# Seams and one product: a vision kernel whose setup work is moved and whose first MLP product takes its variance another way

## The reference

```python
x = x + block0(groupnorm(x)); x = x + block1(groupnorm(x))
# block 0: windowed attention, then an MLP with a depthwise 5x5 convolution
y   = layernorm(tok) * norm1_w + norm1_b             # over the 96 channels of each pixel
tok = attention(y) + tok                             # 16x16 windows, step 14, 4 heads
...
y = (x2 - mean(x2)) / sqrt(var(x2) + 1e-5) * norm2_w + norm2_b   # over 96 channels
y = gelu(y @ fc1_w + fc1_b)                          # 96 -> 192
y = y + gelu(depthwise_conv5x5(y) + dw_b)
x1 = y @ fc2_w + fc2_b + x2                          # 192 -> 96
# block 1: each pixel of a region joins the nearest of 4 centres in each of 4 heads
f, v = conv1x1(x1, f_w), conv1x1(x1, v_w)
...
out = conv1x1(weighted per-head mean of v over each centre's pixels, spread back, proj_w)
```

## Time and profile before

| | us |
|---|---|
| median of 3 runs | 6937.62 (6933.67 to 6956.9) |
| the profiled execution, its own time | 6937.03 |
| its span | 6935.3 |
| PE busy in the span | 6015.5 (87%) |
| DVE busy | 5209.9 (75%) |
| ACT busy | 3497.3 (50%) |
| POOL busy | 2286.0 (33%) |

### The profile page before, as it was taken

The page is one execution under the profiler, slowest core; times in us unless marked ns, Lnnn a source line. Parts: engine busy times, 40 slices in busy tenths (PEclk is TensorE's granted clock), DMA queues, the critical chain, the costliest instruction groups (busy, mean ns, idle before and its releaser), DMA issues. The chain is left out here.

```text
span 6935.3 us, 135783 instructions
## 1 busy us (share of the span) xinstructions
PE 6015.5 (87%) x51768; PEld 3118.6 (45%) x51768; DVE 5209.9 (75%) x7712; ACT 3497.3 (50%) x5182; POOL 2286.0 (33%) x4080
## 2 busy tenths in 40 slices
PE   0885999999999999999999689989998666578887
PEld 0332555555555555555555233335555111066663
DVE  7686888888888888888888455558887445456666
ACT  0553666666666666666666356644443111144431
POOL 0343455555554555555554656610000000000000
PEclk9997999999999999999999799999999788789987
DMA  7786344444444444444443598888987999835667
GB/s 306 192 240 179 72 106 101 101 104 106 103 108 100 103 109 102 105 101 101 107 96 71 146 269 235 237 288 345 345 341 266 283 314 316 249 90 167 189 183 248
DMA packets 761666, 1252.65 MB, mean 181 GB/s; under 512 B 159364, under 2 KB 477828, under 8 KB 730948
## 3 DMA queue, kind: packets, MB, share of 16 engines
q1 hardware_dynamic: 700532, 1090.77, 55.8%
q10 hardware_dynamic: 54560, 111.50, 5.3%
q0 software_dynamic: 5936, 41.68, 1.7%
HBM read 680.81 MB, written 508.40 MB: 171 GB/s over the span
## 5 line engine op out<-in xcount | busy, mean ns | idle before, releaser
L801 DVE TENSOR_REDUCE at_mz<-at_ps 128x4 bf16<-128x1024 f32 x1444 | 1772.3, 1227 | 105.3 <-PE at_ps L720 80.3
L668 ACT ACTIVATE at_E<-at_ps 128x1024 f32<-128x1024 f32 x1444 | 1399.4, 1021 | 382.6 <-PE at_ps L732 368.0
L732 PE MATMUL at_ps<-at_qaug,at_k 32*128 32x256 f32 x11552 | 830.0, 401 | 23.7 <-DVE at_qaug L842 23.7
L743 PE MATMUL at_ps<-at_E,at_vaug 128*32 128x256 f32 x11552 | 774.3, 385 | 5.5
L1282 PE MATMUL cv_ps<-cv_yin,cv_band 128*128 128x384 f32 x2304 | 745.4, 486 | 26.2 <-DMA cv_yin<-y_mlp 26.2
L1302 DVE TENSOR_TENSOR cv_yin<-cv_gl,cv_yin 64x384 f32<-64x384 f32 x1152 | 637.6, 553 | 150.3 <-ACT cv_gl L1293 142.4
L732 PEld LDWEIGHTS at_ps<-at_qaug,at_k 32*128 32x128 f32 x11552 | 523.0, 184 | 494.1 <-issue 384.5
L590 POOL TENSOR_TENSOR at_share<-at_rden,t_share 128x8 f32<-128x8 f32 x722 | 148.5, 206 | 1445.5 <-DVE at_rden L812 1445.5
L1282 PEld LDWEIGHTS cv_ps<-cv_yin,cv_band 128*128 128x128 f32 x2304 | 436.1, 189 | 335.7 <-DMA cv_yin<-y_mlp 27.1
L720 PE MATMUL at_ps<-at_k,at_q 32*128 32x256 bf16 x5776 | 574.2, 275 | 8.9 <-DMA at_k<-at_packed 7.4
L1293 ACT ACTIVATE cv_gl<-cv_ps,cv_bias 128x384 f32<-128x384 f32 x576 | 335.1, 582 | 435.8 <-PE cv_ps L1282 435.8
(11 more groups left out here) (217 smaller groups left out, 9596.0 us busy)
## 6 DMA issues: line engine op xcount, KB each, us to landing
cv_yin<-y_mlp SPq DMA_DIRECT2D x48, 2340.0 KB, 14.8
s_mlp<-cv_yin SPq DMA_DIRECT2D x48, 2340.0 KB, 8.4
at_rows_in<-y_attention SPq DMA_DIRECT2D x76, 768.0 KB, 6.1
gn_xin<-in_x SPq DMA_DIRECT2D x16, 3072.0 KB, 23.2
ln_xin<-in_x SPq DMA_DIRECT2D x192, 256.0 KB, 7.4
y_attention<-ln_xin SPq DMA_DIRECT2D x192, 256.0 KB, 3.8
cl_xu<-x SPq DMA_DIRECT2D x128, 384.0 KB, 3.6
at_xr<-in_x SPq DMA_DIRECT2D x68, 672.0 KB, 5.7
```

The costliest lines, as they stand in the source:

```text
L668: act.activation(E[:, m % 2, 2 * p:2 * p + 2, :], psum[:, 2 + 2 * p:4 + 2 * p, :], ACT.Exp).then_inc(exp_done, 1)
L732: i = pe.matmul(psum[:, 2 + h, TOK * j:TOK * j + TOK], k[rows, n % 2, tokens(w, 128 * j, 128)], qaug[rows, m % 2, :], start=True, stop=True)
L743: i = pe.matmul(pv_ps[32 * h:32 * h + VC, 0:TOK], vaug[:, m % 2, z, h, :], E[:, m % 2, h, z * TOK:(z + 1) * TOK], start=(z == 0), stop=(z ...
L801: dve.tensor_reduce(mz[:, m % 2].rearrange("p j (h c) -> p h j c", c=32)[:, 2 * p:2 * p + 2, :, DQ], psum[:, 0:2, :].rearrange("p h (j n) ...
```

## The change

At the start, the statistics use the norm's ring (six buffers, `norm_tables`), the norm's first four tiles are loaded into it by the statistics' queue, the weights are loaded on ScalarE's queue meanwhile, the first image's aggregation comes right after its tiles, and scale and shift are spread by three matmuls with a spread identity instead of 24 transfers. In `fc1` the weights' loads move to ScalarE's queue; the weights are centred once (each column's mean over the channels is subtracted), so that x needn't be; the mean comes from one matmul on the sum of the three slices, made by VectorE; POOL squares the raw x; and the variance is the mean square less the squared mean, which ScalarE makes. In `fc2` the final waits go (the next block's sync engine waits instead), and the setup's loads and memsets run there on POOL's queue; `cluster_setup` makes the centres in 8 VectorE instructions and 8 POOL copies, and shares the last copies with ScalarE and POOL.

```diff
@@ group_norm_statistics @@
             for m in range(STEPS):
...
-                if m >= NBUF:
-                    sp.wait_ge(taken, m - NBUF + 1)
+                if m >= XB:
+                    sp.wait_ge(taken, m - XB + 1)
+                sp.dma_start(xin[:, m % XB, :], src[:, part * CH:(part + 1) * CH]).then_inc(loaded[m % XB], 16)
+            for k in range(LN_AHEAD):
+                sp.wait_ge(taken, STEPS + k - XB + 1)
+                norm_load(sp, x, s, k)
...
+            act.wait_ge(cleared, 4)
+            for to, of in setup_weights(p, t, s):
+                act.dma_start(to, of).then_inc(s["weights_loaded"], 16)
...
-            dve.wait_ge(taken, STEPS)
-            for b in range(B):
-                n = PART * PER
-                dve.bn_aggr(t["mean_var"][:, b, :], stats[:, b * n:(b + 1) * n, :]).then_inc(aggregated, 1)
+                if m % PART == PART - 1:
+                    b, n = m // PART, PART * PER
+                    dve.wait_ge(taken, m + 1)
+                    dve.bn_aggr(t["mean_var"][:, b, :], stats[:, b * n:(b + 1) * n, :]).then_inc(aggregated, 1)
@@ attention_setup @@
+            for grp in range(CGRP):
+                m = pe.matmul(ps[:, 3, 4 * grp:4 * grp + 2 * B], s["spread"][:, grp, :], t["gn"][:].rearrange("p a b -> p (a b)"), start=True, stop=True)
...
+                link(dve.tensor_copy(s["affine"][half], ps[half, 3, 0:4 * CGRP].rearrange("p (s a b) -> p a s b", a=2, b=B)[:, :, :, b]))
@@ layer_norm @@
-            for grp in range(CGRP):
-                for g in range(4):
-                    for to, of in ((scale, t["gn_scale"]), (shift, t["gn_shift"])):
-                        sp.dma_start(to[32 * g:32 * g + 32, grp:grp + 1], of[32 * grp:32 * grp + 32, g // 2:g // 2 + 1]).then_inc(w_loaded, 16)
...
-            for k in range(AHEAD):
-                load(k)
@@ new @@
+def norm_load(queue, x, s, k):
+    i = (k + GN_TILES) % XB
+    for grp in range(CGRP):
+        for g in (0, 2, 1, 3):
+            queue.dma_start(s["xin"][32 * g:32 * g + 32, i, grp, :], norm_rows(x, k, g, grp)).then_inc(s["loaded"][i], 16)
@@ fc1, gpsimd @@
-                pool.wait_ge(cen_done, n + 1)
+                if n == first[2 * k]:
+                    pool.wait_ge(loaded[k % XB], 16 * LOADS * (k // XB + 1))
                 if n >= 2:
                     pool.wait_ge(var_done, n - 1)
@@ fc1, tensor @@
+            for grp in range(CGRP):
+                m = pe.matmul(mean_ps[:, 0:MLP], ones[:], w1[:, grp, :], start=(grp == 0), stop=(grp == CGRP - 1))
+            m.then_inc(b_done, 1)
...
+                pe.wait_ge(total_done, 2 * n + 2)
                 if n:
-                    pe.wait_ge(cen_done, n)
-                for grp in range(CGRP):
-                    m = pe.matmul(mean_ps[:, 0:w], ones[:], part(x, n, grp), start=(grp == 0), stop=(grp == CGRP - 1))
-                m.then_inc(mean_done, 1)
+                    pe.wait_ge(msq_done, n)
+                pe.matmul(mean_ps[:, 0:w], ones[:], total[:, n % 2, 0:w], start=True, stop=True).then_inc(mean_done, 1)
@@ fc1, scalar @@
+            def squared_mean(n):
+                w = chunks[n][2] * W
+                act.wait_ge(mean_done, n + 1)
+                if n >= 2:
+                    act.wait_ge(var_out, 2 * (n - 1))
+                act.activation(msq[:, n % 2, 0:w], mean_ps[:, 0:w], ACT.Square).then_inc(msq_done, 1)
...
                 for i, (a, b) in enumerate(pairs):
+                    if a is not None:
+                        squared_mean(a)
                     if b is not None:
                         gelu(b)
@@ fc1, vector @@
+            dve.wait_ge(b_done, 2)
+            for grp in range(CGRP):
+                dve.tensor_tensor(w1[:, grp, :], w1[:, grp, :], mean_ps[:, 0:MLP], ALU.subtract).then_inc(w_set, 1)
...
-            def centred(n):
...
-                dve.tensor_tensor(part(x, n), part(x, n), m, ALU.subtract).then_inc(cen_done, 1)
+            def totalled(n):
...
+                dve.tensor_tensor(to, part(x, n, 0), part(x, n, 1), ALU.add).then_inc(total_done, 1)
+                dve.wait_ge(total_done, 2 * n + 1)
+                dve.tensor_tensor(to, to, part(x, n, 2), ALU.add).then_inc(total_done, 1)
 
             def variance(n):
...
                 dve.wait_ge(var_done, n + 1)
-                dve.tensor_copy(rs[:, v % 3, b0 * W:(b0 + count) * W], var_ps[:, 0:count * W]).then_inc(var_out, 1)
+                dve.wait_ge(msq_done, n + 1)
+                dve.tensor_tensor(r, var_ps[:, 0:count * W], m, ALU.max).then_inc(var_out, 1)
+                dve.wait_ge(var_out, 2 * n + 1)
+                dve.tensor_tensor(r, r, m, ALU.subtract).then_inc(var_out, 1)
...
                     if a is not None:
-                        centred(a)
+                        totalled(a)
                         if a:
                             variance(a - 1)
@@ fc2 @@
-            for u in range(XA):
-                sp.wait_ge(stored[u], 16 * XLOADS * len(range(u, NTILE, XA)))
+        @block.gpsimd
+        def _(pool):
+            for to, of in setup_loads(p, t, s):
+                pool.dma_start(to, of).then_inc(s["loaded"], 16)
@@ cluster_setup @@
+            pool.wait_ge(stage, 4)
+            for q in range(NREG):
+                pool.tensor_copy(xmq[:, q].rearrange("p e (i j) -> p e i j", j=2),
+                                 quarters(xm, q).unsqueeze(1).to_broadcast([C + 1, CH_HEADS, 2, 2])).then_inc(spread_done, 1)
+            for b in range(B):
+                pool.tensor_copy(t["rhs"][:, 4 * b:4 * b + 4, 0:2 * C], wfv[:, b, :].unsqueeze(1).to_broadcast([C + 1, 4, 2 * C])).then_inc(spread_done, 1)
...
-                for e in range(CH_HEADS):
-                    link(dve.tensor_scalar(ctr[:, q, e, :].rearrange("p (i j) -> p i j", j=2), quarters(cn), heads[:, e:e + 1], None, ALU.mult))
-                    link(dve.tensor_copy(xmq[:, q, e, :].rearrange("p (i j) -> p i j", j=2), quarters(xm)))
+                last = dve.tensor_tensor(ctr[:, q].rearrange("p e (i j) -> p e i j", j=2),
+                                         quarters(cn, q).unsqueeze(1).to_broadcast([C, CH_HEADS, 2, 2]),
+                                         heads[:].unsqueeze(2).unsqueeze(3).to_broadcast([C, CH_HEADS, 2, 2]), ALU.mult)
```

355 lines of the change are left out of this document (191 added, 164 removed).

## The result

The changed kernel takes 6960.98 us (median of 10 runs, 6947.41 to 6970.84) where the kernel before, beside it, takes 6938.42 (10 runs): ratio 1.0026, 95% interval 1.0014 to 1.0039. That is 22.6 us slower (+0.33% of the medians); the forecast was 46 us slower, 6984. The direction and the main mechanism were right, the size was not: it is half of the forecast. The profiled execution of the changed kernel took 6970.84 (span 6969.0), so 34 us more than the profiled one before; 11 of the 34 are chance of these two executions, and the last stage, whose instructions no run changes, takes from 818 to 835 us in the profiled executions.

A forecast was written before the change was run, and what follows sets the result against it. Each stage between barriers was taken to have its own limit, TensorE in fc1. 6937 - 41 (start) + 115 (fc1) - 27 (end) = 6984 us; the forecast's own range 6955 to 7015, for all cases 6825 to 7015.

The forecast's parts named there:

- The term for fc1: First product of the MLP: 115 us longer, bounds -110 to +150.
- the start's gain: Statistics to norm: the norm starts at 143.9 instead of 184.96, 41 us saved, bounds 28 to 44.
- the end's gain: fc2's landing wait and the setup before the clusters: 27 us saved, bounds 18 to 30.
- The main step: fc1: VectorE instructions with two SBUF inputs and POOL's exclude each other, TensorE idles 3.3 us a slot, its clock falls.
- Rival (b): fc1: after POOL's square VectorE runs its instructions without POOL between; chain 8.4 us, total 6827; chance 0.24.
- Rival (c): fc1: no exclusion at all for short instructions; slots of 7.7 us, -80, total 6790; chance 0.06.
- the walk: fc1's full slot followed instruction by instruction: 10.95 us between variances, a quad 102.6 instead of 90.9, +59 over five.
- Rival (a): fc1: the exclusion acts but TensorE's clock holds; total 6928; chance 0.18.
- Rival (d): Start: its loads land late while fc1 behaves as forecast; total 7000; chance 0.06.
- The clock: fc1: TensorE's clock falls after six pauses per quad, 8 in 10 costing 1.7 us: 8.2 per quad, +41.
- Ten of eleven pauses: TensorE: of eleven pauses above 2.5 us read, ten lowered the clock, each costing about 1.7 us.
- Its issue waits only for the eleventh tile, near 95 us: Start: the first norm tile is issued near 95 us and there near 134, before it is wanted.

The follow-up runs named there:

- e1: The changed kernel with fc1 as before, so only start and end changed: 6865.14 us, 72.8 under the kernel before, ratio 0.9887.
- e7: The kernel before with the changed end alone (fc2's queues and the setup): 6895.6 us, 43.6 under the kernel before, ratio 0.9931.
- e4: The changed kernel with VectorE's two adds of a chunk put ahead of the older chunk's normalisation: 6905.66 us, ratio 0.995.
- e5: The changed kernel with the mean by three matmuls on raw x and VectorE's two adds left out: 6869.0 us, 70.2 under the kernel before.
- e6: The changed kernel with the square of x on ScalarE instead of GpSimd: 6930.86 us, 8.4 under the kernel before.
- e12: The changed kernel with one more GpSimd add per chunk, from the fifth on, whose result nobody reads: 6999.06 us, 60.9 over the kernel before.
- e9: The changed kernel with unused matmuls filling TensorE's pauses before each mean, from the fourth v on: 6967.54 us, 29.4 over the kernel before.
- e8: The changed kernel with two of the norm's four early tiles issued in the norm's own stage: 6952.55 us, 13.3 over the kernel before.
- e13: The kernel before with unused tables of the setup's size ahead of fc2's buffers: 16.7 us under the kernel before.
- e16: The kernel before with a 192-byte pad a partition, putting fc2's x buffer on a multiple of 256 bytes: 18.3 us under the kernel before.
- e10: e7 with the setup's 18 loads put back on the sync engine's queue: 28.3 us under the kernel before.

## Why the prediction came out as it did

The sign and the mechanism were forecast; what failed is the size of all three terms of the sum, and the errors partly cancel. The term for fc1 was 19 us too high, the start's gain 12 too high because the sync engine's own issues were priced at nothing, and the end's gain 17 too low because the place of fc2's buffers was not in it.

| part | forecast | measured |
|---|---|---|
| start | -41 | -29.2 (e1 less e7); -29.7 in the profile |
| fc1 | +115 | +95.8 (after less e1); +95.3 in the profile |
| end | -27 | -43.6 (e7) |
| sum | +47 | +23.0; the changed kernel itself +22.6 |

**The main step held.** The product is slower because VectorE's instructions with two SBUF inputs and GpSimd's take turns, the chain of a slot ends in T2, TensorE waits for it and the clock falls in part of the pauses. Each link was seen, and e4, e5, e6 and e12 moved the time in the direction of the theory, though e4, e6 and e12 fell outside the ranges that I expected. Rival (b), VectorE taking its turns in a row, fell: GpSimd's adds stand between S and N and between N and T1. Rival (c), no exclusion for short instructions (where the prediction speaks of the adds that escape, it calls this one "the second rival"), fell: T1 is 0.68 alone and 1.74 there. T2 is the exception, 0.69 in both, as the walk had it: nothing of GpSimd's stands beside it. Rival (a), the clock holds, fell: 0.86. Rival (d), late loads at the start, did not occur: what was late was the issuing, not the data.

**The term for fc1 was too large by 19 us.** Its parts: the five steady quads were to cost 59 for the walk and 41 for the clock, together 100; they cost 73. The clock: I took six pauses of 3.3 us in a quad, 8 in 10 of them slow at 1.7, 8.2 us; e9 gives back 5.5. The walk: 102.6 forecast, 105.8 less 5.5 is 100.3. Chunk 0 to chunk 22 cost 25.3 where I took 15, and the stage's start gave 2.9 where I took 0. So no mechanism was missing in fc1, but the pauses were not what I forecast: only two of a quad are 3.1 us, two are 8.6, and four groups of ten are slow, one of them after 1.95 us. "Ten of eleven pauses", from which I took 8 in 10, was read from the norm and from fc1 outside its steady part.

**A step that was wrong: the start.** "Its issue waits only for the eleventh tile, near 95 us" is true of the first tile's twelve issues of 48. I priced the data's arrival and the barrier by VectorE, and put the sync engine's own instructions at nothing; they take 53 us and also stand before the barrier. It cost 11 to 12 us; e8 took 9.5 of them back at the setup.

**A step that was missing: the place of fc2's buffers.** The forecast priced the end at 27, and its own terms were right: 24.9 for the setup, 5 for the waits. The other 14 are fc2's: 17 come of the shift alone in e13 and 18 of the pad in e16, but only 6 are left in e10. The tables made earlier moved the x buffer by 7104 bytes; that this acts through alignment is likely and stays open. Nothing in the profile of before points there except that fc2's DMA engines are busy all the time; that a change moves buffers could have been read from the diff.

With the measured sizes in place of the forecast ones, 12 more for the start, 19 less for fc1 and 17 less for the end, the forecast's +47 becomes 47 + 12 - 19 - 17 = +23. That the direction came out is the mechanism; that the time came within 23 us of the forecast owes something to errors of both signs.

## What to carry to other kernels

Price an instruction added on VectorE by what takes turns with it: sum the durations of GpSimd's instructions that read SBUF and of VectorE's with two SBUF inputs over one slot of the pipeline, and put the instruction that others wait for first in that row (e4, 55 us for one swapped order). When an issue of loads is moved ahead of a barrier, count how long the queue holds the issuing engine, since the barrier waits for it. When a stage keeps the DMA engines busy all the time, look where its large buffers start, also when the change is elsewhere, and try a pad of some bytes: here it was worth up to 18 us.

## What the runs showed of the hardware that was not expected

A pad of 192 bytes ahead of one buffer, which then starts on a multiple of 256 bytes, made the whole kernel 18.3 us faster (0.26%, interval 0.14 to 0.39%); the stage of that buffer, in which the DMA engines are always busy, took 671.8 us instead of 685.0. A GpSimd add that nobody waits for, in GpSimd's idle time, cost 38 us; a memset of about the same length 13, by way of the clock. A VectorE maximum against a constant, 512 elements from SBUF to SBUF, takes 0.43 us where it waits for nothing and 2.35 as median beside GpSimd's square, although it has one tensor input. TensorE's clock fell after a pause of 3.06 us in one slot and held after 3.07 in another slot of the same quad.
